# Spreading the dst keys over rows in a GNN kernel's rank rounds: one fp32 turn of a staged column in place of two bf16 products

## What is computed

```python
def _L0_gnn_ref(m, vals, Wn, bn, Ws, bs, rows, cols):     # 3 hops
    H = m
    for i in range(3):
        msg = H[cols] * vals[:, None]
        Hn = segment_sum(msg, rows, num_segments=N)
        H = (Hn @ Wn[i].T + bn[i]) + (H @ Ws[i].T + bs[i])
        if i != 2:
            H = elu(H)
    return H
x = _layernorm(x + _L0_gnn_ref(x, edge_weight, ..., src, dst))
x = _layernorm(x + _L1_gnn_ref(x, ..., edge_attr_3, [src, dst]))   # attention over the edges of each dst, 8 heads
```

## Time and profile before

| | us |
|---|---|
| median of 3 runs | 3001.64 |
| lowest, highest | 2999.54, 3003.59 |
| the profiled execution, its own time | 3012.79 |
| span of its trace (first to last instruction) | 3011.0 |

### The profile page before, as it was taken

How to read it: one execution, slowest core, us unless ns; L and a number is a source line. 1 busy time by engine, 2 the same in 40 slices (tenths; PEclk the granted TensorE clock), 3 DMA queues, 4 the chain that set the end, 5 groups by cost and what they waited for, 6 DMA issues and landing times.

```text
span 3011.0 us, 40665 instructions
## 1 busy us (share of the span) xinstructions
PE 2305.8 (77%) x10293; PEld 1444.1 (48%) x10294; DVE 1471.4 (49%) x3883; ACT 607.0 (20%) x1667; POOL 1634.0 (54%) x1365
## 2 busy tenths in 40 slices
PE   0067443899999999999999999975566655664993
PEld 0055333577777644444444444444344443443772
DVE  2268999577777500000000111065565555667888
ACT  1021000022222100000001000012222222225994
POOL 1157777777777154444444442025555555545995
PEclk9987555555555699999999999987776677776997
DMA  9621221112121255444443445325555555554983
GB/s 382 239 22 1 0 0 0 0 1 0 0 0 0 69 148 144 131 116 139 133 136 108 136 131 163 113 81 169 171 156 165 161 163 162 164 155 143 270 267 113
DMA packets 297611, 350.47 MB, mean 116 GB/s; under 512 B 105434, under 2 KB 223921, under 8 KB 294961
## 3 DMA queue, kind: packets, MB, share of 16 engines
q1 hardware_dynamic: 205825, 247.70, 27.1%
q0 software_dynamic: 91696, 101.74, 16.5%
HBM read 242.39 MB, written 106.86 MB: 116 GB/s over the span
## 4 chain that ended last, share of the span: by engine, by line
PE 62%; issue 12%; DVE 11%; another core or an unknown queue 7%; SPq 4%; ACT 1%; DVEq 1%; DMA 0%; ACTq 0%; POOL 0%
PE psum L889 26%; PE psum L792 7%; PE psum L1006 7%; DVE found L1323 5%; PE psum L961 4%; PE psum L777 3%; SPq L447 2%; PE psum L799 2%; PE psum L737 2%; PE psum L643 2%; PE psum L878 2%; PE psum L766 1%; PE psum L952 1%; DVE acc L1557 1%
## 5 line engine op out<-in xcount | busy, mean ns | idle before, releaser
L578 POOL DMA_INDIRECT adjacency<-total,place x392 | 613.4, 1565 | 336.7 <-DVE total L1334 139.8
L585 POOL DMA_INDIRECT rows_by_dst<-rec,place x392 | 376.7, 961 | 501.4 <-PE psum L889 475.5
L599 POOL DMA_INDIRECT gath<-gat_rows,rec x416 | 398.5, 958 | 450.0 <-ACT digits L1186 183.3
L889 PE MATMUL psum<-a_t,acc 128*128 128x512 f32 x1200 | 527.1, 594 | 4.7 <-DMA a_t<-adjacency 4.7
L889 PEld LDWEIGHTS psum<-a_t,acc 128*128 128x128 f32 x1200 | 228.6, 191 | 275.3 <-issue 272.6
L961 PE MATMUL psum<-x,acc 128*128 x832 | 298.2, 510 | 65.7 <-DVE acc L1557 48.8
L1323 DVE SCALAR_TENSOR_TENSOR found<-psum,key_f,not_before 128x1024 bf16<-128x1024 f32 (+7 forms) x392 | 293.2, 815 | 0.1
L889 PE MATMUL psum<-a_t,x 128*128 128x512 f32 x600 | 262.2, 592 | 0.0
L961 PEld LDWEIGHTS psum<-x,acc 128*128 128x128 f32 x832 | 199.5, 257 | 130.2 <-issue 90.5
L1557 DVE TENSOR_TENSOR acc<-wT,psum 128x528 f32<-128x528 f32 x208 | 145.7, 700 | 220.4 <-issue 168.6
L792 PE MATMUL psum<-table,ohhiT 32*128 32x128 f32 x784 | 238.9, 457 | 0.3 <-ACT table L1065 0.3
(11 more groups left out here) (282 smaller groups left out, 3018.2 us busy)
## 6 DMA issues: line engine op xcount, KB each, us to landing
a_t<-adjacency SPq DMA_DIRECT2D x450, 256.0 KB
gat_h_by_edge<-gath SPq DMA_DIRECT2D x104, 528.0 KB
gath<-gat_h_by_edge SPq DMA_DIRECT2D x104, 528.0 KB, 4.5
adjacency<-zeros POOLq DMA_DIRECT2D x18, 2178.5 KB, 48.3
gath<-gat_rows,rec POOLq DMA_INDIRECT x416
adjacency<-total,place POOLq DMA_INDIRECT x392
rows_by_dst<-rec,place POOLq DMA_INDIRECT x392
x_in<-in_x SPq DMA_DIRECT2D x1, 3072.0 KB
```

Source lines behind the costliest of these rows:

```text
L578: pool.indirect_dma_start(out=adj, in_=total[:, c:c + 1], out_offset=bass.IndirectOffsetOnAxis(ap=place[:, 0, c:c + 1], axis=0), in_offset ...
L585: pool.indirect_dma_start(out=rows_dst, in_=rec[:, c, :], out_offset=bass.IndirectOffsetOnAxis(ap=place[:, 1, c:c + 1], axis=0), in_offset ...
L599: pool.indirect_dma_start(out=gath[:, g % 4, c % 4, :], out_offset=None, in_=hh_dram, in_offset=bass.IndirectOffsetOnAxis(ap=rec_i[:, c, 0 ...
L889: i = pe.matmul(sums[b], table_g[:, w, b * P:(b + 1) * P], a_t[:, q % NA, 0:width(g)], start=k == 0 and g < OWN_GROUPS and w == 0, stop=w ...
```

## The change

The two bf16 products of a column are replaced by one fp32 transpose of the unsplit key. For this a ring of two slots, `dst_st`, is added, and DVE copies the 8 columns of a group from `dst_f` into it, once per group, directly behind the low one-hots of that group. TensorE waits for this copy (`s_dst`) ahead of the spread; the explicit nop ahead of it is gone. Before the loop, the first copy stands behind the first low one-hots. `hi_d`, `lo_d` and `ident_w` are still made.

```diff
+        dst_st = sb("dst_st", [P, 2, U], F32, work)
...
+        s_dst = sem("dst_keys_staged")
...
-            def spread(t, s, n, cold):
+            def spread(t, p, s, n, cold):
...
                 if not cold:
                     pe.wait_ge(s_rank, n - 1)
-                    pe.nop(nofuse=True)
+                pe.wait_ge(s_dst, t + 1)
                 for j in range(4):
-                    for part, eye in ((hi_d, ident_w), (lo_d, identb)):
-                        col = part[:, bass.ds(t * U + 4 * s + j, 1), 0:1].rearrange("p c k -> p (c k)")
-                        i = pe.matmul(rows[:, j * P:(j + 1) * P], col.broadcast_to([P, P]), eye[:, :],
-                                      start=part is hi_d, stop=part is lo_d, skip_group_check=True)
+                    i = pe.transpose(rows[:, j * P:(j + 1) * P],
+                                     dst_st[:, p, 4 * s + j:4 * s + j + 1].broadcast_to([P, P]), identf[:, :])
                 i.then_inc(s_drow, 1)
...
-                    ahead = iter(()) if last and s else spread(t + s, 1 - s, n + 1, first and s == 0)
+                    ahead = iter(()) if last and s else spread(t + s, (p + s) % 2, 1 - s, n + 1, first and s == 0)
...
                     low_onehots(t + 1, 1 - p)
+                    v.tensor_copy(dst_st[:, 1 - p, :], dst_f[:, bass.ds((t + 1) * U, U)]).then_inc(s_dst, 1)
...
             low_onehots(0, 0)
+            v.tensor_copy(dst_st[:, 0, :], dst_f[:, 0:U]).then_inc(s_dst, 1)
             ranks(0, 0, True)
```

More of the change, by code:

```diff
@@ L802, in rank_step @@
                         next(ahead, None)
-            for _ in spread(0, 0, 0, True):
+            for _ in spread(0, 0, 0, 0, True):
                 pass
```

## The result

| | before | with the change |
|---|---|---|
| median of 20 runs, us | 3001.91 | 3008.47 |
| lowest, highest | 2992.47, 3008.70 | 3000.72, 3015.33 |
| span of the profiled execution | 3011.0 | 3007.5 |

The ratio of the runs is 1.0023, 95% interval 1.0014 to 1.0032: the change costs 6.6 us, 0.2%, with 4 to 10 us in the interval. The forecast was 3010.2 us, with 3002 to 3018.

The account below looks back on a forecast made before the run. TensorE at half clock was taken to bound the rank rounds: 97 halves at 0.075 us (7.3) plus 1.3 us for the first round give 8.6 us on 3001.64, so 3010.2 us, range 3002 to 3018.

Parts of the forecast that it names:

- What bounds: Rank rounds: TensorE alone bounds them, at clock 0.50, with 98 halves of 4.34 us making a 425 us stage.
- Halving the instructions saves nothing: Spread of a half: one fp32 transpose streams in 0.21 us, the time of two bf16 products at 0.107 each.
- The piece of 1.04 us in place of 0.97, 0.075 a half: TensorE from first L777 to L792: four transposes take longer than eight products, 7.3 us over 97 halves.
- the rival of half the cost: Spread: open load or border smaller by 0.03 to 0.05 us a half, giving 3006 us; chance 19%.
- The border stays when both sides are fp32: Last L777 to L792: 0.14 us beyond streaming remains with an fp32 transpose before an fp32 product.
- the rival with free borders: L777 to L792: fp32 transpose passes to fp32 product without the 0.14 us, giving 2996 or 2991 us; chance 6%.
- the shape rule: L777 to L792: the extra 0.14 us was laid to the stationary operand changing from 128 by 128 to 32 by 128.
- The weight load: Transposes' 0.230 us loads hide behind the matmul ahead; only the first is open, by 0.05 us.
- The first round, 1.3 us late: Start of the rank rounds: TensorE waits for the first staged copy, so L792 follows 1.3 us later, once.
- The copy and the wait in the loop are covered: VectorE's 49 copies and TensorE's wait cost nothing, with 5.7 us of slack; if not covered, 12 us.
- The clock: Rank rounds: stays at 0.50; the rival grants TensorE 2.4 GHz, some 50 us less, 2950 us; chance 2%.
- no change that can be told: Whole kernel: measured time within 0.2% (6 us) of the kernel before; chance 25%.

Follow-up runs that it names:

- twice: The changed kernel with the four transposes of a half issued two times: stage 514.2 us against 431.4; median 2924.97, ratio 1.0337 to the kernel before.
- early_copy: The changed kernel with the first copy of staged keys moved ahead of the windows' one-hots: 2837.84 us against 2829.91 for the kernel before, ratio 1.0028.
- copy_only: The changed kernel with the eight bf16 products back in place of the four transposes, copy and wait kept: 2830.27 us against 2829.91 before, ratio 1.0003.
- narrow_product: The changed kernel with four plain fp32 products of 32 columns ahead of a half's transposes: stage 393.3 us, ratio 0.9888 to the kernel before.
- before_fill4: The kernel before with four narrow fp32 products ahead of a half's eight bf16 products: 2786.27 us against 2829.16, ratio 0.9848, stage 374.0 us.

## Why the prediction was right, point by point

- *What bounds.* TensorE alone, at 0.50 of its clock. Shown by twice (0.853 us a half for four transposes of 0.213) and by the stage's length, which for one kernel is the same on every chip that was traced.
- *Halving the instructions saves nothing.* Right: a transpose takes 0.213 us, like two bf16 products.
- *The piece of 1.04 us in place of 0.97, 0.075 a half.* Measured 1.05 and 0.080. All of the four distances were right to 0.01: 0.27, 0.21, 0.21, 0.35; the rest is the rounding of the rows. It is the traces that exclude the rival of half the cost (0.03 a half): by the times alone, its 4 us lie at the edge of the interval.
- *The border stays when both sides are fp32.* Right, and the rival with free borders fell. The row that it was argued from was misread, though: the 1.06 us of the earlier trace rows hold one border and not two, since they begin with the start of L643. The opened load makes the first distance 0.32 in place of 0.22, and the border behind L643 is 0.31 - 0.22 = 0.09 us at 2.4 GHz. The conclusion that fp32 beside fp32 pays a border doesn't change by it. Its reason was put too widely: it isn't the shape of the operand but what part of the array is used. Had the kernel's narrow operations been fp32 transposes, the shape rule would have given a wrong number.
- *The weight load.* Right: 0.230 us each, with only the first one open. The rule on fast weight loads had no price here, since a load hides behind the matmul ahead.
- *The first round, 1.3 us late.* Measured 1.3 against the start of the round's work (2.74 us in place of 1.48), of which early_copy gets 1.2 back. By the clock of the trace the first L792 came only 0.4 us later, and SP's first load at 1037.95 where 1038.4 was forecast: these two signs took for granted that the stage is reached at the same time, and it was reached 0.8 us earlier.
- *The copy and the wait in the loop are covered.* Shown by copy_only, stage 423.7 us. VectorE's wait for L792 stays.
- *The clock.* It stayed at 0.50, as forecast. But I wrote that nothing speaks for a rise, on the ground of equal full-width work; narrow_product and before_fill4 had the same full-width work in a half, beside the narrow products, and the clock rose. The 2% for this case came from a reason that doesn't hold; that the clock stayed is in part luck. Nor does it stay at 0.50 in all of the pair rounds, as the prediction has it: from 200 to 275 us it was mostly 1.00, as the earlier trace rows show for the first slices too, and full-rate transposes lie there. That transposes keep the full clock away is not borne out by this case.
- *The sum,* 8.6 us, against 9.0 in the trace and 6.6 (4 to 10) in the times. The chance of 25% for "no change that can be told" was fair: the interval reaches below 6 us.

## What to carry to other kernels

Count a TensorE edit in streaming time and in changes of the part of the array that is used, not in instructions: one fp32 transpose streams like two bf16 products (0.213 us at 1.2 GHz), and from the last start of a group to the next operation it takes 0.106 us more, since its own stream is that much longer than one product's. If a key doesn't fit bf16, ask first whether an offset makes it fit fp16. And where TensorE is busy all the time at half its clock, the clock is worth an experiment, since it may be a larger term than any product. Such a gain then hangs on a clock that no run here explains.

## What was not expected of the hardware

- Changing the part of the array that is used (all of it, 32 columns, 32 rows) costs 0.13 to 0.14 us at 1.2 GHz (0.32 us from the first bf16 update to a full-width operation, 0.18 to 0.19 to one in the same tile). By the same reading each half of the rank rounds pays it five times: from the table reads to the updates twice, into and out of the spread, and from the one-hot turns to the table reads.
- An fp32 transpose with 32 columns behaves as an untiled one; an fp32 product with 32 columns doesn't.
- TensorE busy for 100 us of 100 was granted 1.2 GHz for the whole stage in ten of the kernels; four small fp32 products more in each half brought 2.4 GHz for most of it to two others, and took 50 us off the stage of 424 in the kernel before.
